# Reordering the last part of a four-layer network's first layer, and moving one group's channel scaling to ScalarE

## Chip, cores and metric

One Trainium2 chip, one core of it. The metric is the device time of one execution in microseconds, as the median of several runs.

## What is computed

The input x is 16 images of 64 channels and 16x16 pixels, float32. Four blocks follow one another, each as x = x + block(norm(x)), where norm is a group norm over pairs of channels:

```python
x = x + L0(gn(x))   # two dynamic convolutions, a 1x1 projection, channel and spatial attention
x = x + L1(gn(x))   # efficient attention and a three-level pyramid of channel attentions
x = x + L2(gn(x))   # 3x3 and 1x1 convolution mix
x = x + L3(gn(x))   # area attention, depthwise 5x5 and projection
```

The change lies in the last part of L0 and the first part of L1. The end of L0, after the second dynamic convolution (its product is y2):

```python
h = silu(bn2(y2))                       # 128 channels
h = silu(bn3(proj_w @ h))               # h3, 64 channels
a = sigmoid(mlp(mean(h)) + mlp(max(h))) # one number per image and channel: "channel gate"
h = h * a                               # h4
s = concat(mean over channels, max over channels)
x = x + h * sigmoid(conv7x7(s))         # one number per image and pixel: "map"
```

L1 begins with the norm, then products for keys, queries and values, exponentials, and two further levels of the image as differences of Gaussian blurs ("pyramid").

## The kernel before

An image pair is a tile t of 128 partitions (2 images x 64 channels) by 256 pixels; there are 8 tiles. They form two groups g = 0, 1 of four tiles, and within a group jj = 0, 1 counts two tiles (j = 2g + jj). Every engine has its own program, and all are written by walking one list, `SCHEDULE`: a list of steps such as `("h4T", jj, g)`, and every engine executes its own part of the step, if it has one, in that order. The list is built from `CHAIN`, in which group 1 runs three steps behind group 0. So the order of the list is the order of work on each engine, and an engine that waits in one step holds back all later steps on that engine. Nothing reorders at run time.

The steps around the change, with the parts of the engines and their lines:

- `y2` (L426, L1256): TensorE product of the second convolution; ScalarE silu (L1261) into h2.
- `y3` (L436, L921, L1264): TensorE projection (L442); ScalarE silu with a sum (L1267) into h3; VectorE maximum over pixels (L924).
- `mlp1` (L446, L927), `mlp2` (L454, L1278): the MLP's first product (L451), VectorE relu and add (L932, L935), second product (L457), ScalarE tanh (L1280) into `cag`.
- `h4T` (L460, L937): VectorE finishes the gate, 0.5 + 0.5 tanh (L942, with jj = 0 only), scales h3 by it (L945) into h4; TensorE transposes h4 to pixel-major (L468); VectorE sums and maxima over channels (L952).
- `conv7` (L471, L955, L1283): VectorE scales the sums (L958, `mean4`); TensorE multiplies by a 7x7 convolution as a matrix (L478); ScalarE tanh (L1285).
- `add` (L482, L960): TensorE spreads the map over channels (L413); VectorE adds to X (L964, L967) and takes the statistics of the next norm (L798, with jj = 1 also L805).
- `norm` 1: TensorE pair means (L353); VectorE variance (`gn_variance`, L814 to L816); POOL power -0.5 (L1470); VectorE coefficient (L824) and apply (L832) into xn1. `later_norm` (L839) puts these together.
- `in1` (L487, L1071, L1345): TensorE transposes (L495), keys (L498), queries and values (L505); VectorE maximum of the keys (L980), tokens (L1002), L994, L1012, L1013; ScalarE copy (L1298) and exponentials (L1293, L1313, L1327).
- `pyramid` (L509, L1316): sixteen 512-wide passes on TensorE (L517), copies on ScalarE (L1321).

TensorE's results go to PSUM banks in two rings, six for large and two for small products; `claim` (L330) takes the next bank and waits for the reader of what it held. The order of the claims is the order of the steps.

Part of the list before, from the first step that the change moves:

```python
("y2",0,1) ("mlp1",0) ("y3",0,1) ("mlp2",0) ("y2",1,1) ("h4T",0,0) ("y3",1,1) ("h4T",1,0)
("mlp1",1) ("conv7",0) ("mlp2",1) ("add",0,0) ("h4T",0,1) ("add",1,0) ("h4T",1,1) ("norm",1,0)
("conv7",1) ("in1",0,0) ("add",0,1) ("in1",1,0) ("add",1,1) ("pyramid",0) ("norm",1,1)
```

Of the kernel before, what the change touches and what calls it, by code (L numbers as in the profile page):

```python
# [25 lines left out]
NG = NP // 2  # L26
# [64 lines left out]
SCHEDULE = []  # L91
# [7 lines left out]

del SCHEDULE[SCHEDULE.index(("het", 0, 0)):]
SCHEDULE += [(*step, 1) for step in CHAIN[CHAIN.index(("norm", 2)) - LAG + 1:CHAIN.index(("norm", 2))]]
SCHEDULE += [("norm", 2, 1), ("het", 0, 0), ("het", 1, 0), ("norm", 3, 0), ("het", 0, 1), ("start3",), ("het", 1, 1)]
# [15 lines left out]
def program(nc, x_in, const_in, weight_in, param_in, out):  # L120
    F32 = mybir.dt.float32
    ALU = mybir.AluOpType
    ACT = mybir.ActivationFunctionType
# [8 lines left out]
    with ExitStack() as ctx:  # L132
# [8 lines left out]
        def bank(n, a=0, b=512):  # L141
            return psum[:, n * 512 + a:n * 512 + b]
# [29 lines left out]
        def sm(cols):  # L172
            small_bytes[0] += cols
            assert small_bytes[0] <= 1200
            return small[:, small_bytes[0] - cols:small_bytes[0]]
# [12 lines left out]
        mlp_s, cag = sm(NP), sm(NP)  # L188
# [21 lines left out]
        def pairs(cols=HW, layout="p (t n) -> p t n", axis=1, **sizes):  # L210

            n = NG * cols
            take(n)
            assert used[0] <= AREA_COLS // 2
            return ByGroup([region[:, at:at + n].rearrange(layout, t=NG, **sizes)
                            for at in (used[0] - n, AREA_COLS // 2 + used[0] - n)], axis)
# [6 lines left out]
        xs0, hs1, h3, h4, x_add = (pairs() for _ in range(5))  # L223
# [14 lines left out]
        xn1 = pairs()  # L238
# [12 lines left out]
        mix, mix2 = e_l[0], e_l[1]  # L251
# [527 lines left out]
        def _(dve):  # L779
            v = nc.vector  # L780
# [15 lines left out]
            def gn_stats(l, t, src_sem, value):  # L796
                dve.wait_ge(src_sem, value)
                v.bn_stats(stats[l][:, t, :], X[:, t, :]).then_inc(dve_small, 1)  # L798
                small_n[0] += 1
                stats_at[(l, t)] = small_n[0]  # L800

            def gn_aggr(l, g):
                for t in range(4 * g, 4 * g + 4):
                    dve.wait_ge(dve_small, stats_at[(l, t)])
                    v.bn_aggr(mv[l][:, t, :], stats[l][:, t, :]).then_inc(gn_mv[g], 1)  # L805
# [13 lines left out]
            def gn_coefs(l, g):  # L819
                dve.wait_ge(gn_pow[g], l + 1)  # L820
                n = where[("gn", l, g)]
                avg = bank(n, 0, 8).rearrange("p (t s) -> p t s", t=4)
                c = slice(4 * g, 4 * g + 4)
                v.scalar_tensor_tensor(out=gn_nb[l][:, c], in0=avg[:, :, 0], scalar=-1.0, in1=gn_rs[l][:, c],  # L824
                                       op0=ALU.mult, op1=ALU.mult).then_inc(gn_coef[g], 1)

            def gn_apply(l, t, dst):
                dve.wait_ge(gn_coef[t // NG], l + 1)
                src = X[:, t, :]
                if len(dst.shape) == 3:  # L830
                    src = src.rearrange("p (y x) -> p y x", y=W)
                v.tensor_scalar(dst, src, gn_rs[l][:, t:t + 1], gn_nb[l][:, t:t + 1], ALU.mult, ALU.add)\  # L832
                    .then_inc(xn_ready[t // NG], 1)
# [11 lines left out]
            def norm(l, g):  # L845
                if l == 0:
                    for t in range(NG * g, NG * (g + 1)):
                        gn_stats(0, t, x_loaded[t // 2], 16)
                    gn_aggr(0, g)
                    gn_variance(0, g)  # L850
                    gn_coefs(0, g)
                    c = slice(NG * g, NG * (g + 1))
                    v.tensor_tensor(xmean[:, c], gn_d[0][:, c], gn_rs[0][:, c], ALU.mult).then_inc(xmean_ready, 1)
                    for t in range(NG * g, NG * (g + 1)):
                        gn_apply(0, t, xn0[:, t, W:W + HW])
                elif l == 1:
                    later_norm(1, g, lambda t: xn1[:, t, :])
                elif l == 2:
                    dve.wait_ge(zero_ready, 2)
                    later_norm(2, g, lambda t: xn_pad[:, t, 1:17, 1:17])  # L860
                else:

                    dve.wait_ge(y1out_mm, NP)
                    later_norm(3, g, lambda t: xn3[:, t, :])
# [62 lines left out]
            def channel_mlp1(g):  # L927
# [6 lines left out]
                dve.wait_ge(mlp1_ready, 2 * g + 1)  # L934
                v.tensor_tensor(mlp_s[0:8, c], mlp_r[0:8, 0, c], mlp_r[0:8, 1, c], ALU.add).then_inc(mlp1_ready, 1)  # L935

            def tokens4(jj, g):  # L937
                j = 2 * g + jj
                if jj == 0:
                    own = cag[:, NG * g:NG * (g + 1)]  # L940
                    dve.wait_ge(cag_tanh, g + 1)
                    v.tensor_scalar(own, own, 0.5, 0.5, ALU.mult, ALU.add).then_inc(cag_ready, 1)  # L942
                dve.wait_ge(cag_ready, g + 1)
                for t in (2 * j, 2 * j + 1):
                    v.tensor_scalar(h4[:, t, :], h3[:, t, :], cag[:, t:t + 1], None, ALU.mult).then_inc(h4_ready, 1)  # L945

                dve.wait_ge(h4T_mm, j + 1)
                src = bank(where[("h4T", j)]).rearrange("p (q k b c) -> p q k b c", q=2, k=NK, b=2)
                for ch, op in ((0, ALU.add), (1, ALU.max)):
                    for q in range(2):  # L950
                        t = 2 * j + q
                        last = v.tensor_reduce(sT[:, ch, :, 2 * t:2 * t + 2], src[:, q, :, :, :], X_AXIS, op)  # L952
                    last.then_inc(sT_part, 1)

            def mean4(g):  # L955
                dve.wait_ge(sT_part, 4 * (g + 1))
# [222 lines left out]
            def add_out3(t):  # L1179
                dve.wait_ge(y3out_mm, t + 1)  # L1180
                dve.wait_ge(xt_ready, t + 1)
                if t >= 4:
# [3 lines left out]
                    .then_inc(yout_ready, 1)  # L1186

            steps = {"norm": norm, "ctx": context, "gate": gates, "spread": map_input,
                     "later_weights": later_weights, "y3": pool_max, "mlp1": channel_mlp1, "h4T": tokens4,
                     "conv7": mean4, "add": add0, "in1": in1, "levels": levels1, "scores1": scores1, "mix": mix1,  # L1190
                     "out1": out1, "het": het, "start3": first_keys}
            for name, *at in SCHEDULE:
                if name in steps:
# [3 lines left out]
            for w in range(NT + STEPS_MORE):  # L1197
                t, r = divmod(w, 4)
                j, r8 = divmod(w, 8)
# [25 lines left out]
        def _(act):  # L1225
            a = nc.scalar
# [51 lines left out]
            def channel_gate(g):  # L1278
                act.wait_ge(mlp2_mm, g + 1)
                a.activation(cag[:, NG * g:NG * (g + 1)], bank(where[("mlp2", g)], 0, NG), ACT.Tanh, scale=0.5)\  # L1280
                    .then_inc(cag_tanh, 1)

            def spatial_gate(g):  # L1283
                act.wait_ge(conv7_mm, g + 1)
# [134 lines left out]
            def second_blocks(l, g):  # L1419
                if l == 2:  # L1420
                    rows_of_groups(g, (2, 3))

            steps = {"norm": second_blocks, "gate": gates, "taps": taps_out, "conv": input_gate, "y1": silu1, "y2": silu2, "y3": silu3,
                     "mlp2": channel_gate, "conv7": spatial_gate, "in1": in1, "pyramid": pyramid_out,
                     "levels": levels1, "levels_T": levels_T, "scores1": scores1, "het": het_out, "start3": start3}
            for name, *at in SCHEDULE:
                if name in steps:
# [2 lines left out]
            for w in range(NT + 2):  # L1430
                j, r8 = divmod(w, 8)
# [301 lines left out]
```

## Time and profile before

| | |
|---|---|
| runs | 302.39, 304.10, 303.56 us; median 303.56 |
| profiled execution: time | 303.56 us |
| its span, first to last instruction | 301.8 us |
| TensorE busy | 228.6 us (76%) |
| VectorE busy | 187.1 us (62%) |
| ScalarE busy | 128.6 us (43%) |
| GpSimd (POOL) busy | 35.9 us (12%) |
| mean granted clock of TensorE | 0.869 of full |
| chain that ended last | PE 51%, DVE 23%, ACT 7%, issue 7%, DMA 5%, POOL 4% |

PE is TensorE's products, PEld its weight loads, DVE VectorE, ACT ScalarE. A busy share is an average over the whole span. The chain that ended last is followed back from the last instruction, at each step to what released it.
### The profile page before, as it was taken

Reading aid. Unit: us, or ns where it says so; the run is one execution under the profiler, and the core shown is the slowest. Engines: PE = TensorE matmul, PEld = TensorE weight load, DVE = VectorE, ACT = ScalarE, POOL = GpSimd, SP = SyncE. Lnnn points to the kernel's source line nnn. Section 1 sums busy time; section 2 is a strip of 40 time slices with the busy share of each in tenths; the row PEclk is TensorE's granted clock in tenths of the full one; section 3 lists DMA queues with packets and bytes.
Section 4 is the critical chain, followed back from the end, with each engine's and each line's share of the span. In section 5 each row is a group of like instructions: output and inputs, shape, how many; then the busy total and the mean of one; then the engine's idle time right before and its main releaser. Section 6 shows DMA issues by size and latency. Waiting matters only on the chain.

```text
span 301.8 us, 5842 instructions
## 1 busy us (share of the span) xinstructions
PE 228.6 (76%) x2192; PEld 133.9 (44%) x2192; DVE 187.1 (62%) x525; ACT 128.6 (43%) x322; POOL 35.9 (12%) x64
## 2 busy tenths in 40 slices
PE   0479897384399869988453679469989998988954
PEld 0355663132266546777321122234554564463541
DVE  3562343717449798398793036676497697697772
ACT  1025579400045577899300113336585465552410
POOL 1750000000100100000005022066020020000000
PEclk9996999855579999999755699958999999997995
DMA  7900000000000000000059951552034024100010
GB/s 231 393 0 3 0 2 1 0 0 2 0 0 0 3 0 0 2 3 2 1 138 211 217 121 36 129 120 67 0 80 101 2 66 117 45 6 21 0 37 35
DMA packets 9644, 16.54 MB, mean 55 GB/s; under 512 B 1936, under 2 KB 8208, under 8 KB 9360
## 3 DMA queue, kind: packets, MB, share of 16 engines
q1 hardware_dynamic: 8848, 13.58, 16.6%
q10 hardware_dynamic: 768, 2.58, 4.1%
q8 instruction: 18, 0.29, 0.4%
q14 instruction: 10, 0.08, 0.1%
HBM read 4.71 MB, written 1.05 MB: 19 GB/s over the span
## 4 chain that ended last, share of the span: by engine, by line
PE 51%; DVE 23%; ACT 7%; issue 7%; DMA 5%; POOL 4%; ACTq 2%; SPq 0%; DVEq 0%; POOLq 0%
PE psum L671 7%; PE psum L517 5%; PE psum L699 4%; DMA region<-xn_pad 4%; PE psum L717 4%; PE psum L689 3%; PE psum L651 3%; DVE xn_pad L1142 3%; DVE smax L1148 3%; POOL small L1470 2%; PE psum L478 2%; PE psum L413 2%; PE psum L505 2%; PE psum L633 2%; PE psum L388 2%
## 5 line engine op out<-in xcount | busy, mean ns | idle before, releaser
L1405 ACT ACTIVATE region<-psum 128x512 f32<-128x512 f32 x32 | 19.0, 593 | 32.7 <-PE psum L699 32.6
L1148 DVE TENSOR_REDUCE smax<-psum 128x8 f32<-128x512 f32 x32 | 21.8, 682 | 13.0 <-PE psum L689 13.0
L1470 POOL TENSOR_TENSOR small<-small 128x4 f32<-128x4 f32 x8 | 8.1, 1018 | 169.5 <-DVE small L816 169.5
L671 PE MATMUL psum<-region,w 128*32 128x512 f32 x160 | 22.6, 636 | 4.1 <-DVE region L1123 4.1
L1399 ACT ACTIVATE region<-region 128x512 f32<-128x512 f32 x32 | 20.1, 627 | 12.1 <-DVE region L1155 12.0
L798 DVE BATCH_NORM_STATS2 small<-X 128x6 f32<-128x256 f32 x32 | 12.5, 422 | 18.2 <-ACT X L1275 17.0
L699 PEld LDWEIGHTS psum<-const,region 128*128 128x128 f32 x128 | 14.9, 149 | 18.2 <-issue 12.1
L699 PE MATMUL psum<-const,region 128*128 128x128 f32 x128 | 21.9, 297 | 1.1 <-ACT region L1405 1.0
L1155 DVE TENSOR_TENSOR region<-psum,smax 128x512 f32<-128x512 f32 x32 | 22.0, 686 | 0.6
L717 PE MATMUL psum<-region 128*64 128x18 f32 x512 | 20.6, 214 | 0.0
L717 PEld LDWEIGHTS psum<-region 128*64 128x64 f32 x512 | 17.5, 138 | 5.4 <-issue 5.4
L1275 ACT ACTIVATE X<-psum,small 128x256 f32<-128x256 f32 x8 | 3.4, 470 | 37.2 <-PE psum L633 37.2
L633 PE MATMUL psum<-region,weight 128*32 128x512 f32 x96 | 12.7, 667 | 7.2 <-DMA region<-xn_pad 7.0
L651 PE MATMUL psum<-region,weight 128*128 128x512 f32 x24 | 13.9, 676 | 2.6 <-DVE small L824 2.6
L353 PE MATMUL psum<-small,const 128*128 128x8 f32 x16 | 4.0, 325 | 14.2 <-DVE small L805 10.0
L517 PE MATMUL psum<-region,const 128*128 128x512 f32 x32 | 14.2, 598 | 0.0
L1142 DVE SCALAR_TENSOR_TENSOR xn_pad<-v_pad,small,xn_pad 128x256 f32<-128x256 f32 x32 | 14.0, 483 | 0.0
L1285 ACT ACTIVATE region<-psum 8x256 f32<-8x256 f32 x2 | 0.7, 374 | 27.9 <-PE psum L478 27.9
L353 PEld LDWEIGHTS psum<-small,const 128*128 128x128 f32 x16 | 3.7, 284 | 17.5 <-DVE small L805 12.8
L689 PE MATMUL psum<-region 32*64 32x256 f32 x256 | 10.3, 433 | 1.3 <-ACT X L1275 1.3
L1298 ACT ACTIVATE region<-psum 128x512 f32<-128x512 f32 x20 | 11.0, 624 | 0.7 <-PE psum L495 0.7
L1518 POOL COPY region<-v_pad 128x256 f32<-128x256 f32 x16 | 6.3, 436 | 40.9 <-PE psum L660 37.1
(166 smaller groups left out, 472.5 us busy)
## 6 DMA issues: line engine op xcount, KB each, us to landing
region<-v_pad SPq DMA_DIRECT2D x64, 80.0 KB, 2.1
region<-xn_pad SPq DMA_DIRECT2D x16, 157.5 KB, 7.3
region<-xn_pad ACTq DMA_DIRECT2D x16, 157.5 KB, 7.2
weight<-weight_in SPq DMA_DIRECT2D x1, 1376.0 KB, 10.6
const<-const_in SPq DMA_DIRECT2D x1, 1170.0 KB, 7.9
X<-x SPq DMA_DIRECT2D x4, 256.0 KB, 4.4
out<-xn_pad SPq DMA_DIRECT2D x8, 128.0 KB, 1.7
weight<-weight_in SPq DMA_DIRECT2D x1, 918.0 KB, 5.0
```

Source lines behind the costliest of these rows:

```text
L517: last = mm(bank(n), lap[s][:, k, jn * 128:(jn + 1) * 128], xT[:, k, 4 * g:4 * g + 4, :].rearrange("p t c -> p (t c)"), start=(k == 0), st ...
L633: last = mm(bank(n)[32 * q:32 * q + 32, :], hetW[:, q % 2, dx, :], rows[:, q, 2 * jj:2 * jj + 2, 0:W, dx:dx + W], start=False, stop=(dx == 2),
L651: mm(bank(n), wt(w), xn3[:, 2 * j:2 * j + 2, :].rearrange("p t n -> p (t n)"), start=True, stop=True)\
L671: last = mm(bank(n)[32 * c:32 * c + 32, :], w4[:, c % 2, dx, :], v4[:, j % 2, c, :, :, dx:dx + W], start=(dx == 0), stop=(dx == 4), tile_p ...
L689: last = mm(bank(banks[r], a2 * 256, a2 * 256 + 256)[64 * c:64 * c + 64, :], q3[rows, j % 2, a, :], km[rows, j % 2, a, :, :].rearrange("p ...
L699: last = tr(bank(n, q * 128, (q + 1) * 128), e3[:, w % NE, q * 128:(q + 1) * 128], ident)
L717: last = mm(dst[half, a2, b, h:h + 2, :].rearrange("p h e -> p (h e)"), e3T[:, w % NE, at + 64 * c:at + 64 * c + 64], va[:, 4 * t + 2 * a2 ...
L1142: v.scalar_tensor_tensor(out=a, in0=win, scalar=pe_w[:, 5 * PE_ROWS + i:5 * PE_ROWS + i + 1], in1=prev, op0=ALU.mult, op1=ALU.add).then_in ...
L1148: v.tensor_reduce(smax[:, w, :], src, X_AXIS, ALU.max).then_inc(smax_ready, 1)
L1155: v.tensor_tensor(s_sub[:, w % NE, :].rearrange("p (h m) -> p h m", h=HEADS), src, smax[:, w, :].unsqueeze(2).broadcast_to([P, HEADS, AP_] ...
L1399: a.activation(e3[:, u % NE, :], s_sub[:, u % NE, :], ACT.Exp, scale=HD ** -0.5).then_inc(e3_ready, 1)
L1405: a.activation(e3T[:, u % NE, :], bank(where[("e3T", u)]), ACT.Copy).then_inc(e3T_ready, 1)
```

## The change

The 23 steps from `("y2", 0, 1)` up to `("levels", 0, 0)` get a new order by hand. The steps before and after keep theirs. In the new order both MLP steps of group 0 stand together and ahead of y2 of jj = 1, group 0's transposes, map product and both adds are ahead of group 1's transposes, `in1` of jj = 0 is ahead of group 1's map product, and group 1's adds stand together ahead of the pyramid.

On VectorE the gate's affine step moves from `h4T` to the step `mlp2`. `h4T` of group 0 scales and sums as before; of group 1 it does nothing on VectorE. The scaling of group 1 moves to ScalarE (`second_scaled`, four Copy activations with the gate as scale). The channel sums of group 1 and its `mean4` move into VectorE's part of `("norm", 1, 0)`: sums of jj = 0, then the variance, sums of jj = 1, `mean4`, then coefficient and apply.

```diff
--- before.py
+++ after.py
@@ -99,6 +99,12 @@
 
 
 
+TAIL = [("y2", 0, 1), ("mlp1", 0), ("mlp2", 0), ("y2", 1, 1), ("h4T", 0, 0), ("y3", 0, 1), ("h4T", 1, 0), ("y3", 1, 1), ("conv7", 0),
+        ("mlp1", 1), ("mlp2", 1), ("add", 0, 0), ("add", 1, 0), ("h4T", 0, 1), ("h4T", 1, 1), ("norm", 1, 0), ("in1", 0, 0),
+        ("conv7", 1), ("in1", 1, 0), ("add", 0, 1), ("add", 1, 1), ("pyramid", 0), ("norm", 1, 1)]
+first, beyond = SCHEDULE.index(TAIL[0]), SCHEDULE.index(("levels", 0, 0))
+assert sorted(SCHEDULE[first:beyond]) == sorted(TAIL)
+SCHEDULE[first:beyond] = TAIL
 del SCHEDULE[SCHEDULE.index(("het", 0, 0)):]
 SCHEDULE += [(*step, 1) for step in CHAIN[CHAIN.index(("norm", 2)) - LAG + 1:CHAIN.index(("norm", 2))]]
 SCHEDULE += [("norm", 2, 1), ("het", 0, 0), ("het", 1, 0), ("norm", 3, 0), ("het", 0, 1), ("start3",), ("het", 1, 1)]
@@ -853,6 +859,15 @@
                     v.tensor_tensor(xmean[:, c], gn_d[0][:, c], gn_rs[0][:, c], ALU.mult).then_inc(xmean_ready, 1)
                     for t in range(NG * g, NG * (g + 1)):
                         gn_apply(0, t, xn0[:, t, W:W + HW])
+                elif l == 1 and g == 0:
+
+                    map_sums(0, 1)
+                    gn_variance(1, 0)
+                    map_sums(1, 1)
+                    mean4(1)
+                    gn_coefs(1, 0)
+                    for t in range(NG):
+                        gn_apply(1, t, xn1[:, t, :])
                 elif l == 1:
                     later_norm(1, g, lambda t: xn1[:, t, :])
                 elif l == 2:
@@ -934,16 +949,21 @@
                 dve.wait_ge(mlp1_ready, 2 * g + 1)
                 v.tensor_tensor(mlp_s[0:8, c], mlp_r[0:8, 0, c], mlp_r[0:8, 1, c], ALU.add).then_inc(mlp1_ready, 1)
 
+            def channel_gate(g):
+                dve.wait_ge(cag_tanh, g + 1)
+                own = cag[:, NG * g:NG * (g + 1)]
+                v.tensor_scalar(own, own, 0.5, 0.5, ALU.mult, ALU.add).then_inc(cag_ready, 1)
+
             def tokens4(jj, g):
+
+                if g == 0:
+                    dve.wait_ge(cag_ready, 1)
+                    for t in (2 * jj, 2 * jj + 1):
+                        v.tensor_scalar(h4[:, t, :], h3[:, t, :], cag[:, t:t + 1], None, ALU.mult).then_inc(h4_ready, 1)
+                    map_sums(jj, 0)
+
+            def map_sums(jj, g):
                 j = 2 * g + jj
-                if jj == 0:
-                    own = cag[:, NG * g:NG * (g + 1)]
-                    dve.wait_ge(cag_tanh, g + 1)
-                    v.tensor_scalar(own, own, 0.5, 0.5, ALU.mult, ALU.add).then_inc(cag_ready, 1)
-                dve.wait_ge(cag_ready, g + 1)
-                for t in (2 * j, 2 * j + 1):
-                    v.tensor_scalar(h4[:, t, :], h3[:, t, :], cag[:, t:t + 1], None, ALU.mult).then_inc(h4_ready, 1)
-
                 dve.wait_ge(h4T_mm, j + 1)
                 src = bank(where[("h4T", j)]).rearrange("p (q k b c) -> p q k b c", q=2, k=NK, b=2)
                 for ch, op in ((0, ALU.add), (1, ALU.max)):
@@ -951,6 +971,10 @@
                         t = 2 * j + q
                         last = v.tensor_reduce(sT[:, ch, :, 2 * t:2 * t + 2], src[:, q, :, :, :], X_AXIS, op)
                     last.then_inc(sT_part, 1)
+
+            def conv7(g):
+                if g == 0:
+                    mean4(0)
 
             def mean4(g):
                 dve.wait_ge(sT_part, 4 * (g + 1))
@@ -1186,8 +1210,8 @@
                     .then_inc(yout_ready, 1)
 
             steps = {"norm": norm, "ctx": context, "gate": gates, "spread": map_input,
-                     "later_weights": later_weights, "y3": pool_max, "mlp1": channel_mlp1, "h4T": tokens4,
-                     "conv7": mean4, "add": add0, "in1": in1, "levels": levels1, "scores1": scores1, "mix": mix1,
+                     "later_weights": later_weights, "y3": pool_max, "mlp1": channel_mlp1, "mlp2": channel_gate, "h4T": tokens4,
+                     "conv7": conv7, "add": add0, "in1": in1, "levels": levels1, "scores1": scores1, "mix": mix1,
                      "out1": out1, "het": het, "start3": first_keys}
             for name, *at in SCHEDULE:
                 if name in steps:
@@ -1280,6 +1304,12 @@
                 a.activation(cag[:, NG * g:NG * (g + 1)], bank(where[("mlp2", g)], 0, NG), ACT.Tanh, scale=0.5)\
                     .then_inc(cag_tanh, 1)
 
+            def second_scaled(jj, g):
+                if g == 1:
+                    act.wait_ge(cag_ready, 2)
+                    for t in (NG + 2 * jj, NG + 2 * jj + 1):
+                        a.activation(h4[:, t, :], h3[:, t, :], ACT.Copy, scale=cag[:, t:t + 1]).then_inc(h4_ready, 1)
+
             def spatial_gate(g):
                 act.wait_ge(conv7_mm, g + 1)
                 a.activation(gate_map[g][0:GB, :], bank(where[("conv7", g)], 0, HW)[0:GB, :], ACT.Tanh, scale=0.5)\
@@ -1421,7 +1451,7 @@
                     rows_of_groups(g, (2, 3))
 
             steps = {"norm": second_blocks, "gate": gates, "taps": taps_out, "conv": input_gate, "y1": silu1, "y2": silu2, "y3": silu3,
-                     "mlp2": channel_gate, "conv7": spatial_gate, "in1": in1, "pyramid": pyramid_out,
+                     "mlp2": channel_gate, "h4T": second_scaled, "conv7": spatial_gate, "in1": in1, "pyramid": pyramid_out,
                      "levels": levels1, "levels_T": levels_T, "scores1": scores1, "het": het_out, "start3": start3}
             for name, *at in SCHEDULE:
                 if name in steps:
```

## Rows read from the trace of the kernel before

**Rows 1.** The cores: span and mean granted clock of TensorE.

```profile
core 0: 301.8 us, clock 0.869
```

**Rows 2.** Chain of waits, 50 to 104 us: start, length (us), what.

```profile
55.01 1.21 ACT region L1267 x4
...
60.32 3.58 PE psum L478 x8
...
64.41 2.03 PE psum L413 x4
...
81.15 3.58 PE psum L478 x8
...
88.66 1.06 PE psum L413 x4
...
94.00 7.06 PE psum L517 x16
```

**Rows 3.** Stretches of 1 us: length; busy PE, PEld, DVE, ACT, POOL; clock; DMA.

```profile
58.00:59.00 1.00, 0.00 (x0) 0.00 (x0) 0.99 (x3) 0.00 (x0) 0.00 (x0) 0.91 0.00 0
86.00:87.00 1.00, 1.00 (x5) 0.48 (x4) 0.09 (x1) 0.98 (x2) 0.00 (x0) 0.94 0.00 0
171.00:172.00 1.00, 1.00 (x12) 0.14 (x7) 0.00 (x0) 0.00 (x0) 0.00 (x0) 0.77 1.09 217
```

**Rows 4.** Timeline from 168 us, TensorE (columns as in rows 5).

```profile
168.26 3.92 PE L633 MATMUL psum<-region,weight 128*32 128x512 f32 x20 [7.02 <-DMA region<-xn_pad]
```

**Rows 5.** Timeline, 50 to 60: start, length, engine, line, what, count, [idle before].

```profile
49.55 1.47 ACT L1261 ACTIVATE region<-psum,small 128x256 f32<-128x256 f32 x3
...
50.38 0.15 DVE L935 TENSOR_TENSOR small<-small 8x4 f32<-8x4 f32 x1
...
51.65 0.38 PE L457 MATMUL psum<-small,weight 8*128 8x4 f32 x2
...
51.96 1.14 PE L434 MATMUL psum<-region 64*128 64x256 f32 x8
...
52.75 1.93 ACT L1261 ACTIVATE region<-psum,small 128x256 f32<-128x256 f32 x4 [0.27 <-PE psum L434]
...
53.25 0.62 DVE L945 TENSOR_SCALAR region<-region,small 128x256 f32<-128x256 f32 x2
...
54.31 1.08 PE L442 MATMUL psum<-region,weight 128*64 128x256 f32 x8
54.42 1.42 DVE L952 TENSOR_REDUCE small<-psum 128x4 f32<-128x256 f32 x4 [0.55 <-PE psum L468]
...
56.25 0.69 DVE L924 TENSOR_REDUCE small<-region 128x2 f32<-128x512 f32 x1 [0.41 <-ACT region L1267]
...
57.34 0.63 PE L468 MATMUL psum<-const,region 128*128 128x128 f32 x4 [1.95 <-DVE region L945]
```

**Rows 6.** Timeline, 60 to 82, VectorE.

```profile
72.40 0.69 DVE L964 SCALAR_TENSOR_TENSOR region<-psum,region 128x512 f32<-128x512 f32 x1 [0.58 <-PE psum L413]
...
74.53 0.36 DVE L805 BATCH_NORM_AGGREGATE small<-small 128x2 f32<-128x6 f32 x4
...
76.40 1.42 DVE L952 TENSOR_REDUCE small<-psum 128x4 f32<-128x256 f32 x4 [1.01 <-PE psum L468]
...
79.43 0.16 DVE L824 SCALAR_TENSOR_TENSOR small<-psum,small 128x4 f32<-128x4 f32 x1 [1.15 <-POOL small L1470]
79.63 1.38 DVE L832 TENSOR_SCALAR region<-X,small 128x256 f32<-128x256 f32 x4
```

**Rows 7.** Timeline, 82 to 92, ScalarE and VectorE.

```profile
86.42 1.28 ACT L1293 ACT_TABLE_LOAD   x1
...
86.91 0.69 DVE L980 TENSOR_REDUCE small<-psum 128x2 f32<-128x512 f32 x1 [5.82 <-PE psum L498]
...
90.21 0.51 ACT L1313 ACTIVATE region<-region,small 128x256 f32<-128x256 f32 x1 [1.03 <-DVE small L995]
...
91.41 0.68 DVE L964 SCALAR_TENSOR_TENSOR region<-psum,region 128x512 f32<-128x512 f32 x1
```

## The prediction

> **What bounds the kernel now.** I read the cores first: the span is 301.8 us [rows 1], the run that was profiled took 303.56 us, which is also the median of the three runs, so 1.76 us lie around the span and a change of the span can be taken off 303.56 directly. Then the chain of waits, from 60 to 102 us [rows 2]. It shows this stage as one serial string with TensorE in most of it: the 7x7 map product of the first group (conv7(0), L478) at 60.32, the spreading of that map (L413) at 64.41, the same map product for the second group at 81.15, and from there TensorE without a break to the end of the pyramid (L517) at 94.00 + 7.06 = 101.06. The next stage starts from the second group's means behind the pyramid on TensorE, so what ends the stage is how soon that unbroken block of TensorE work can begin.
>
> The granted clock is the second thing to see [rows 3]. It drops to 0.50 (1.2 GHz) at about 58.8 (mean 0.91 in that microsecond) and is back at 2.4 GHz at about 86.1. All the products between run at half speed. Before the drop TensorE had mostly been idle; the rise came 4.9 us into the unbroken block (81.15 to 86.06).
>
> Between 66 and 81 us the string goes through VectorE: first group's add, second group's scaling and channel sums, add, sums, norm, each waiting for TensorE in turn [rows 6].
>
> **The sum, part 1: to conv7(0).** Times are of the trace's own clock. The MLP's second product (L457, 0.38) now stands right behind the first: its input is ready at 50.53, so it ends at 50.95 instead of 52.03 behind y3(0,1) [rows 5]. ScalarE is in silus until 51.02, then the gate's tanh, done 51.2. On VectorE the gate's affine step follows (0.2 with its wait, as L935's 0.15), and from the scaling (L945, 53.25) to the first channel sum (L952, 54.42) it is 1.17 us, so the sums could start at 52.6; the transposes queue behind y2(1,1) (1.14, from 50.95 to 52.1), which makes it 52.8, and sums of 1.42 end at 54.2. ScalarE: silu2(1,1), 1.93, ends at 53.2; the two silus of y3(0,1), 1.21 with their reads [rows 2], at 54.45. Pool maximum 0.69, to 55.2. From the start of the scaling at 53.25 to the end of the sums at 55.84 it is 2.6, so jj = 1 is through at 57.8. But y3(1,1) (1.08) is now behind those transposes on TensorE, from 56.3 (the transposes, 0.63, end 1.5 before the sums do) to 57.4; its silus end 0.7 later at 58.1, the maximum at 58.8, the mean at 59.0, conv7(0) starts at 59.07. That is 1.25 earlier than 60.32, where undoing the queue behind the transposes would have allowed 58.
>
> **Part 2: to the first add.** Both MLP products of the second group stood before or beside conv7(0); now both come after it on TensorE. conv7(0) ends at 62.65 (3.58 at the low clock); mlp1 (0.2), VectorE's two small steps (0.45) and mlp2 (0.5, which is what lies between 63.90 and 64.41 [rows 2]) bring the spreading to 63.8 instead of 64.41, its first map done 2.1 later, the add to 65.9 instead of 66.5. Of the 1.25 us, 0.65 is given back. The channel gate of group 1 is a wait on VectorE with the adds queued behind it; its tanh ends at 64.1, and they wait for the spreading until 65.9 anyway: no cost. The map's tanh is ahead of it on ScalarE and done by then.
>
> **Part 3: the scaling on ScalarE.** Four Copy activations with a scale from SBUF, 128x256, SBUF to SBUF. No row shows this form; the nearest is the exponential of the same size, SBUF to SBUF, 0.51 each [rows 7], the other bound is 1.93 / 4 = 0.48 for a silu of that size from PSUM [rows 5]. Four take 2.0 and run from 64.35 to 66.4 while ScalarE has nothing else. TensorE comes to them at 67.95, so up to 0.9 each would cost nothing. VectorE is spared two pairs of 0.6.
>
> **Part 4: adds and sums on VectorE.** One add with its statistics takes 2.13 (72.40 to 74.53) [rows 6]. The two now run on end, since the spreading of jj = 1 ends at 67.95: 65.9 to 70.2, aggregation 0.36, 70.55. Before, the second add only began at 72.40. TensorE meanwhile does the transposes of the second group (0.63 each at the full clock [rows 5], at most twice that at the low one, to 70.5) and the small product of the means, to 71. The first sums take 1.42, to 71.95, variance 0.5 (77.82 to 78.3, where VectorE's 1.15 of waiting for POOL begins), and that wait is now covered by the second sums, 1.42 to 73.9. Mean and coefficient 0.35, apply from 74.3 instead of 79.63: 5.33 earlier. No order on POOL or SP changes, and no DMA is issued by a moved step.
>
> **Part 5: the block on TensorE.** in1(0,0) now goes ahead of conv7(1). It needs two of four applies (1.38 for the four [rows 6]) and 0.1 to reach TensorE, so it starts 0.8 after 74.3, at 75.1; before, the block started at 81.15: 6.05 earlier. The block holds the same instructions, 19.9 us of which 4.9 at the low clock. TensorE counts as the bound if nobody stalls it. VectorE: the keys' product before landed at 86.91, 2.2 after conv7(1)'s end at 84.73, the last 0.8 at full clock; all low makes it 3.0, so 78.1. in1 takes VectorE 4.5 (86.91 to 91.41) [rows 7], plus up to 0.8 of waiting for slow products: 83.4. ScalarE's exponential of the queries then ends at 84.1 and the second map's tanh, which now sits behind it, at 84.5. TensorE wants that map after in1(0,0), conv7(1) and in1(1,0). The first two took 81.15 to 88.66 [rows 2], 7.5; with 0.4 less for the clock (below) they end at 82.2, and in1(1,0) took 94.00 - 1.05 - 89.72 = 3.2: 85.4. Slack 0.9. VectorE takes in1(1,0) from at most 84.4 to 88.9, two adds to 93.1, aggregation 93.5; the pyramid ends at 94.6. Slack 1.1. The banks that the pyramid takes over are read by 86.2 at the latest. So TensorE bounds it.
>
> The clock in the block: the rise came 4.9 us after the start, of which 3.58 was a product with weights 8 columns wide; in another place it came 3.1 us after (TensorE starts at 168.26 [rows 4], rise in the microsecond from 171 [rows 3]) with wide work. Now wide products come first. I take 4.1, half of the 0.8 difference is 0.4 us gained. Bounds: 3.1 gives 0.9 gained. From above, conv7(0) and the spreading ran 6.1 us on end (60.32 to 66.44) with no rise, so 7.5 is possible: 1.3 us lost against 4.9.
>
> As to a rule: the transposes of in1 open the block. The Trainium skill, "TensorE: Matmul & The Clock Gate", Part 4, says that transposes do not engage the full clock as products do. By that the rise would come about 1 us later and the sum be 0.5 us smaller; the trace has transposes at 84.73 inside a low stretch and the rise 1.3 later, which fits both.
>
> And a second rule, on ScalarE: the second map's tanh now stands between exponentials. The trace has one table load, 1.28, ahead of the first exponential [rows 7]. If tanh needs another table, two more loads come in: 84.5 becomes 85.8, TensorE waits 0.4, and the reload falls before the exponential of the second keys, whose bank the pyramid needs at 89.3, so the bound for this is 0 to 0.4 us. I take 0: the tanhs between the silus of this stage already run without a load of their own (the load in [rows 7] is the stage's only one). The Trainium skill, "ScalarE: Activation LUTs", Table sets, has tanh and exp in one set, by which it is 0; no row here shows a tanh after an exponential.
>
> **Sum:** 6.05 + 0.4 = 6.45 us earlier at the end of the pyramid. Nothing after it changes its order, and it all hangs on that chain, so 303.56 - 6.45 = 297.1.
>
> **Rivals.**
> *The clock falls later (B).* TensorE was idle for 1.95 us before 57.34, worked 0.63 and then had only mlp1 before 60.32 [rows 2, 5]; at 58.8 the clock fell. Now y3(1,1) adds 1.08 us there and conv7(0) starts at 59.07. If 2.4 GHz survives to conv7(0)'s end, that takes 1.8 us instead of 3.6 and the small products 0.3 less: 2.1 more gained, 295.0; through the spreading too, 2.9 and 294.2. For it: the work that fills the gap. Against: between 53.8 and 59.1 it still has no more than 1.7 us of work.
>
> *The rise comes late (C).* 7.5 us instead of 4.1 into the block: 1.7 less gained, 298.8. One us late, if transposes do not serve, costs 0.5 (297.6) and lies in the forecast's own range; it has a third of the forecast's chance. VectorE then also gets its products later, but adds still end before the pyramid. For it: the 6.1 us without a rise; against: those were narrow products.
>
> *Slower (D).* The half clock holds through the block. The block is 19.9 - 2.45 = 17.5 us at full clock. It ends at 75.1 + 17.5 + half the low time; it is later than before once the low time passes 17 us; if all is low it ends at 110 and the kernel takes 312.5. The only mechanism that I find with a price above the 6 us gained. Against: every block of wide work here got its clock within 5 us.
>
> *It does not do what it says (E).* The adds could be held by something I read as free (a gate late on ScalarE, scaling far over 0.9 each): the apply stays near 79 and the time within 1.5 us of 303.
>
> **How the numbers follow.** Forecast 0.50, B 0.25, C 0.15, D 0.05, E 0.05. Range: B with the clock bound of 3.1 at the low end, 293.9; C with the 0.9 us by which the runs of before differ, 299.6; the forecast's own range is 296.2 to 298.3. A measurement tells about 0.5% (1.5 us) from no change; faster by more than that are the forecast, B and C and a part of E: 0.92, same 0.03, slower 0.05.
>
> **What would show it.** Right: conv7(0) near 59.1, first add near 65.9, second on its heels, apply near 74.3, in1(0,0) on TensorE near 75.1 and before conv7(1), end of pyramid near 94.6, still three table loads, four activations near 0.5 us between 64 and 67. Wrong: a wait of TensorE for ScalarE's tanh before the spreading of group 1; VectorE's adds ending after the pyramid; a low clock past 80; later stages that take longer than before.

## The result and the profile after

The changed kernel takes 293.45 us (292.95 to 294.38, four runs) beside 303.41 us before: ratio 0.9678, 95% interval 0.964 to 0.9715. That is 10 us saved where 6.5 were forecast, and 0.45 us below the low end of the range. Some executions of a kernel take over 1.5% longer than its fastest; the ratios here leave these out, the medians and ranges of times hold all executions. The profiled execution of the changed kernel took 294.38 us with a span of 292.6 us; its mean granted clock is 0.894 beside 0.869. The page's span line, busy times and chain:

```profile
span 292.6 us, 5842 instructions
...
PE 223.4 (76%) x2192; PEld 132.7 (45%) x2192; DVE 186.3 (64%) x521; ACT 130.5 (45%) x326; POOL 35.9 (12%) x64
...
PE 50%; DVE 24%; ACT 8%; issue 6%; DMA 5%; POOL 4%; ACTq 2%; SPq 0%; DVEq 0%; POOLq 0%
```

TensorE has the same 2192 instructions but is busy for 5.2 us less (223.4 beside 228.6): the same work ran faster. The chain of waits of the changed kernel, 50 to 100 us (start, length, what), the pieces that answer to [rows 2] and to the sum's steps:

```profile
52.09 1.93 ACT region L1285 x4
54.02 1.10 ACT region L1291 x4
...
56.24 1.07 PE psum L474 x4
57.31 1.93 PE psum L448 x8
...
60.77 1.89 PE psum L484 x8
...
64.57 0.70 DVE region L988
...
72.56 0.75 DVE region L838 x2
...
73.35 1.11 PE psum L501 x4
...
78.29 1.82 PE psum L484 x8
...
85.27 7.06 PE psum L523 x16
...
93.13 1.02 POOL small L1500
```

L474 are the transposes of h4, L448 is y3, L484 the map product conv7, L988 the first add, L838 the apply, L501 the transposes of in1, L523 the pyramid. The pyramid ends at 92.33 instead of 101.06. conv7(0) starts at 60.77, no earlier than before, but takes 1.89 us, not 3.58; the first add is at 64.57, the apply at 72.56, and the block starts at 73.35. The granted clock in the four microseconds in which it moves (columns as in [rows 3]):

```profile
56.00:57.00 1.00, 0.76 (x4) 0.69 (x4) 0.36 (x2) 0.00 (x0) 0.00 (x0) 0.63 0.00 0
59.00:60.00 1.00, 0.21 (x2) 0.00 (x0) 0.06 (x1) 0.71 (x3) 0.00 (x0) 0.66 0.00 0
66.00:67.00 1.00, 0.42 (x4) 0.18 (x2) 0.97 (x3) 0.00 (x0) 0.00 (x0) 0.75 0.00 0
76.00:77.00 1.00, 1.00 (x7) 1.00 (x6) 0.76 (x2) 0.40 (x1) 0.00 (x0) 0.63 0.00 0
```

In this execution it falls at about 56.3, under the transposes (1,0) and y3(1,1), which take 1.07 and 1.98 instead of 0.63 and 1.08. It is back at 59.7, ahead of conv7(0), stays through the spreading, falls at 66.5 and rises 3.4 us into the block, at 76.7. Group 1's activations and the table loads on ScalarE (busy, mean ns, idle before):

```profile
L1311 ACT ACTIVATE region<-region,small 128x256 f32<-128x256 f32 x4 | 1.7, 500 | 0.2 <-DVE small L955 0.2
...
L1256 ACT ACT_TABLE_LOAD x1 | 1.3, 1283 | 0.7 <-PEq L1756 0.7
L1276 ACT ACT_TABLE_LOAD x1 | 1.3, 1283 | 1.7 <-PE psum L429 1.7
L1323 ACT ACT_TABLE_LOAD x1 | 1.3, 1283 | 0.0
```

Four at 0.50 each, near the 0.51 of the forecast, and hidden. There are still three loads, though the second map's tanh (81.70) now stands between exponentials (80.36 and 82.86), so a tanh behind an exponential wants none. That is as the Trainium skill has it ("ScalarE: Activation LUTs", Table sets), and now shown.

**A length that can be compared.** The code ahead of the first moved step is unchanged, yet it starts between 46.9 and 49.6 us: near 47 in the three profiles whose mean granted clock over the first 44 us is 1.00, near 49 where it is 0.92. What lies behind the pyramid takes 199.6 to 203.5 us, though nothing is changed there. So the runs below are also read by the tail: from the first silu of y2(0,1) on ScalarE to the end of the pyramid on TensorE. Before it is 49.08 to 101.06, 51.98 us; the forecast made it 45.5 (94.6 - 49.08); the changed kernel has 42.84. Of the kernel before there is one profile, so its tail stands on one execution.

### The profile page after: what moved, and what is told of

The parts are those of the page before. It is cut to its first block, busy times and chain, and to the rows that moved or that the text cites. A ratio compares the mean times of both kernels' runs of the same rounds, so it can differ in the third digit from the quotient of the medians.

```text
span 292.6 us, 5842 instructions
## 1 busy us (share of the span) xinstructions
PE 223.4 (76%) x2192; PEld 132.7 (45%) x2192; DVE 186.3 (64%) x521; ACT 130.5 (45%) x326; POOL 35.9 (12%) x64
## 4 chain that ended last, share of the span: by engine, by line
PE 50%; DVE 24%; ACT 8%; issue 6%; DMA 5%; POOL 4%; ACTq 2%; SPq 0%; DVEq 0%; POOLq 0%
PE psum L677 7%; PE psum L523 5%; PE psum L705 4%; DMA region<-xn_pad 4%; PE psum L723 4%; PE psum L695 3%; PE psum L657 3%; DVE xn_pad L1166 3%; DVE smax L1172 3%; POOL small L1500 2%; PE psum L511 2%; PE psum L639 2%; ACTq L1446 2%; PE psum L429 2%; ACT region L1367 2%
## 5 line engine op out<-in xcount | busy, mean ns | idle before, releaser
L804 DVE BATCH_NORM_STATS2 small<-X 128x6 f32<-128x256 f32 x32 | 12.5, 422 | 18.2 <-ACT X L1299 16.9
L639 PE MATMUL psum<-region,weight 128*32 128x512 f32 x96 | 12.5, 658 | 7.3 <-DMA region<-xn_pad 7.3
L657 PE MATMUL psum<-region,weight 128*128 128x512 f32 x24 | 13.9, 676 | 2.6 <-DVE small L830 2.6
L1328 ACT ACTIVATE region<-psum 128x512 f32<-128x512 f32 x20 | 10.9, 624 | 8.8 <-PE psum L501 8.8
L523 PE MATMUL psum<-region,const 128*128 128x512 f32 x32 | 14.2, 598 | 0.0
L639 PEld LDWEIGHTS psum<-region,weight 128*32 128x32 f32 x96 | 2.9, 120 | 17.1 <-DMA region<-xn_pad 9.7
## 6 DMA issues: line engine op xcount, KB each, us to landing
weight<-weight_in SPq DMA_DIRECT2D x1, 1376.0 KB, 10.9
```

What stands on the lines that cost most here:

```text
L523: last = mm(bank(n), lap[s][:, k, jn * 128:(jn + 1) * 128], xT[:, k, 4 * g:4 * g + 4, :].rearrange("p t c -> p (t c)"), start=(k == 0), st ...
L639: last = mm(bank(n)[32 * q:32 * q + 32, :], hetW[:, q % 2, dx, :], rows[:, q, 2 * jj:2 * jj + 2, 0:W, dx:dx + W], start=False, stop=(dx == 2),
L657: mm(bank(n), wt(w), xn3[:, 2 * j:2 * j + 2, :].rearrange("p t n -> p (t n)"), start=True, stop=True)\
```

## The experiments

What is to be told apart: the order's own gain from the clock's, and the parts of the order from one another. Ratios are against the kernel before on the same chip.

### Clock held by dummy products

```diff
+def keep_busy(n, times):
+    for _ in range(times):
+        mm(bank(n, 256, 512), ident, lap[1][:, 0, :], start=True, stop=True)
...
 n = claim(pe, ("h4T", j), sT_part, 2 * j + 2)
+keep_busy(n, {(1, 0): 4}.get((jj, g), 0))
```

The dummies write the bank that the step has claimed, and the step overwrites it. In the changed kernel there are 4 before the transposes (1,0), 6 before group 0's means and 7 before in1(0,0), 17 in all. In the kernel before there are 3, 5 and 5 before the transposes (1,0), (0,1) and (1,1), 3 before mlp1(1) and 9 before conv7(1). Where a step waited before it claimed its bank, the claim is moved ahead of the wait.

> The kernel before with dummy products in TensorE's idle stretches between 55 and 81 us (3 to 9 products of 128x256 into the bank that the step claims anyway), so that the clock should stay at 2.4 GHz; the result isn't touched. Clock theory (much of the change's gain beyond 6 us is that the 7x7 product and the spreading now run at full clock): all the work between 58.8 and 86.1 that ran at half speed, 1.8 + 1.0 + 0.5 + 1.0 + 0.5 + 1.8 + 0.6 = 7.2 us on the chain, comes back: about 296.3 us. Order theory (the clock is incidental, the order gave it all): the dummies cost a little and return nothing, 303 to 305 us.

296.72 us, ratio 0.9788 (0.9752 to 0.9823), 6.2 us under the kernel before on that chip. Its profile has no half clock in the tail, which is 45.40 us.

> The changed kernel with dummy products in TensorE's idle stretches before the transposes (1,0), before the means and before in1(0,0). Clock theory: transposes and y3(1,1) at 56 to 59 us (1.4 us too long) and the first 3.1 us of the block (1.5 us too long) run at full clock, 290.6 us; and the distance to filled_before, 5.7 us, is then the order's own share. Order theory: at or above the changed kernel's 293.4 us.

290.08 us, ratio 0.958 (0.9535 to 0.9626), tail 39.98.

> filled_after once more, beside the others on one chip, 289.5 to 291 us: the changed kernel with dummy products in three idle stretches of TensorE. Clock theory: tail 39.9 us with no half clock in it.

291.60 us, ratio 0.9682 (0.9646 to 0.9718), tail 39.98 again. The clock in four microseconds that were low in a profile of the changed kernel or in that of the kernel before:

```profile
53.00:54.00 1.00, 1.00 (x5) 0.57 (x3) 0.77 (x2) 0.20 (x2) 0.00 (x0) 1.00 0.00 0
58.00:59.00 1.00, 1.00 (x7) 0.44 (x5) 0.00 (x0) 0.00 (x0) 0.00 (x0) 1.00 0.00 0
66.00:67.00 1.00, 0.93 (x5) 0.88 (x6) 1.00 (x5) 0.00 (x0) 0.00 (x0) 1.00 0.00 0
70.00:71.00 1.00, 0.79 (x5) 0.69 (x6) 0.80 (x3) 0.10 (x1) 0.00 (x0) 1.00 0.00 0
```

> filled_after without the four dummies before the transposes (1,0). Clock theory: of the 2.9 us, only the 1.5 of the block's first stretch is had in executions where the clock falls at 56 us (those lose up to 1.3), all of it in the others: 290 to 292 us, tail 41.4 us if the profile shows the half clock before conv7(0), 39.9 if not. If the dummies after the spreading don't matter: 293.4 us and tail 42.8.

290.85 us, ratio 0.9675 (0.9624 to 0.9725), tail 39.99 in a profile without half clock in it.

With the clock held the change saves 45.40 - 39.98 = 5.4 us. The clock costs the kernel before 51.98 - 45.40 = 6.6 us of its tail and the changed kernel 2.9. So 3.7 of the 9.1 us of the tail are clock; with the tail of after_third below (41.97) they are 4.6 of 10.0. The times of the two filled kernels, taken on one chip, are 6.6 us apart (296.72 and 290.08), 1.2 more than their tails; that part lies outside the tail and is not explained. The order theory, by which the dummies return nothing, is out for the kernel before. For the changed kernel the gain of the dummies alone is seen in the tail only: its runs without them are of other chips, and the ratios of the three filled versions (0.958, 0.9682, 0.9675) reach up to its own 0.9678. The one comparison on one chip is at the end of the experiments, with conv7(1) moved.

### Which work sits ahead of conv7(0)

```diff
-("h4T", 1, 0), ("y3", 1, 1), ("conv7", 0)
+("y3", 1, 1), ("h4T", 1, 0), ("conv7", 0)
```

> The changed kernel with y3(1,1) ahead of the transposes (1,0). By order alone, the wait of y3 behind the transposes goes and conv7(0) starts 1.1 us earlier: 292.3 us. Clock theory: TensorE's back-to-back stretch at 56 to 59 us, which brought the clock up again at 59.4, is gone, so conv7(0) and the spreading run at half clock (1.8 + 1.0 us more): 294 to 295 us, with the clock at 0.50 under conv7(0) in the profile.

297.24 us, ratio 0.9808 (0.9773 to 0.9843); conv7(0) takes 3.45 us; tail 44.64.

> y3(1,1) ahead of the transposes (1,0), second profile. If TensorE's back-to-back stretch ahead of conv7(0) is what holds or brings the clock: conv7(0) at the half clock again, 3.5 us, tail 44 to 46 us, time 2 to 4 us above after_third. If it was luck: 1.9 us under conv7(0), a tail near 42 and the time of after_third.

296.66 us, ratio 0.9839 (0.9773 to 0.9905); tail 44.99. TensorE's timeline of this one. Between the 2.4 us without work and the 1.7 us ahead of conv7(0) stand only the transposes, 0.63 us, where the changed kernel has y3(1,1) as well:

```profile
52.53 1.95 PE L448 MATMUL psum<-region,weight 128*64 128x256 f32 x16
56.91 0.63 PE L474 MATMUL psum<-const,region 128*128 128x128 f32 x4 [2.44 <-DVE region L962]
59.26 3.58 PE L484 MATMUL psum<-weight,small 128*8 128x256 f32 x8 [1.72 <-DVE small L982]
```

> The changed kernel as it is, once more, for a second profile and six more times. If the clock's pattern in the tail is fixed by the work, the profile shows the same fall near 56 and rise near 59; if it depends on how the execution happens to lie against the clock's steps (my theory, after map_first had none of it in the same code), it shows another, and the times spread over 2 us or so around 293.4 us.

294.42 us (291.51 to 298.00), ratio 0.9705 (0.9637 to 0.9774); conv7(0) 1.89 us; tail 42.83.

> The changed kernel, third profile. If the full clock under conv7(0) is the rule: conv7(0) takes 1.9 us and the tail 41.5 to 42.9 us, time 292 to 294.5 us. If it was luck: 3.5 us and a tail of 44.5 to 46 us in this one.

293.29 us, ratio 0.9716 (0.9651 to 0.9781); tail 41.97. Here the clock does not even fall at 56; y3 behind the transposes is followed by conv7(0) at 1.7 us distance (TensorE's timeline):

```profile
52.44 0.66 PE L474 MATMUL psum<-const,region 128*128 128x128 f32 x4
53.03 1.08 PE L448 MATMUL psum<-region,weight 128*64 128x256 f32 x8
56.32 0.63 PE L474 MATMUL psum<-const,region 128*128 128x128 f32 x4 [2.21 <-DVE region L962]
56.88 1.08 PE L448 MATMUL psum<-region,weight 128*64 128x256 f32 x8
59.64 1.89 PE L484 MATMUL psum<-weight,small 128*8 128x256 f32 x8 [1.68 <-DVE small L982]
```

So in three of three profiles the changed kernel has conv7(0) at the full clock and in two of two the swap has it at half, with the time 3.4 us higher on the same chip (296.66 beside 293.29). It is not certain in each execution. Ten profiles of this section and the next ones have the changed kernel's order up to conv7(0) and no dummies ahead of it; in nine conv7(0) takes 1.89 us, and in the tenth, sums_first below, it is at half:

```profile
55.74 0.63 PE L474 MATMUL psum<-const,region 128*128 128x128 f32 x4 [2.20 <-DVE region L962]
56.30 1.97 PE L448 MATMUL psum<-region,weight 128*64 128x256 f32 x8
59.83 3.48 PE L484 MATMUL psum<-weight,small 128*8 128x256 f32 x8 [1.56 <-DVE small L982]
```

The swap was also a test of my reading that y3(1,1) is held up by the transposes. conv7(0) starts 10.2 us into the tail, where after_third has 10.08: nothing is gained. VectorE's timeline in y3_first_again shows why: the second maximum (L939) is now ahead of the scaling (L962) that the transposes wait for, and it waits for a silu until 55.82.

```profile
54.73 0.69 DVE L939 TENSOR_REDUCE small<-region 128x2 f32<-128x512 f32 x1 [0.67 <-ACT region L1291]
55.82 0.69 DVE L939 TENSOR_REDUCE small<-region 128x2 f32<-128x512 f32 x1 [0.41 <-ACT region L1291]
56.42 0.61 DVE L962 TENSOR_SCALAR region<-region,small 128x256 f32<-128x256 f32 x2
...
65.90 0.69 DVE L988 SCALAR_TENSOR_TENSOR region<-psum,region 128x512 f32<-128x512 f32 x1 [1.54 <-PE psum L419]
```

The last line is the first add. It starts 65.90 - 49.06 = 16.8 us into the tail, to which the half clock through conv7(0) and the spreading brings it; the forecast's sum, made with that clock, had 16.8 too.

### The parts

The first kernel is the one before with the change's list and nothing else:

```diff
+TAIL = [("y2", 0, 1), ("mlp1", 0), ("mlp2", 0), ("y2", 1, 1), ("h4T", 0, 0), ("y3", 0, 1), ("h4T", 1, 0), ("y3", 1, 1), ("conv7", 0),
+        ("mlp1", 1), ("mlp2", 1), ("add", 0, 0), ("add", 1, 0), ("h4T", 0, 1), ("h4T", 1, 1), ("norm", 1, 0), ("in1", 0, 0),
+        ("conv7", 1), ("in1", 1, 0), ("add", 0, 1), ("add", 1, 1), ("pyramid", 0), ("norm", 1, 1)]
```

> The kernel before with the new order of the 23 steps and nothing else: VectorE keeps group 1's scaling, and its sums stand in h4T, ahead of the norm. Against the changed kernel VectorE's string gets two scalings (0.6 each), two waits for transposes (0.5 to 1.0 each) and the POOL wait (1.15) back: 4 to 5 us, so 297.5 to 298.5 us. If the scaling and the sums are incidental and the order gave it all: 294 us.

303.67 us (299.67 to 308.11), ratio 0.9953 (0.9908 to 0.9999), tail 53.16. The profile is of an execution of 304.71 us, and the twelve go down to 299.67, so 53.16 may be a long tail for this kernel; the ratio is the safer measure. A miss, and the expectation had left something out. TensorE and VectorE:

```profile
77.87 1.12 PE L501 MATMUL psum<-const,region 128*128 128x128 f32 x4 [3.82 <-DVE region L838]
...
80.48 3.45 PE L511 MATMUL psum<-weight,region 128*128 128x128 f32 x16
86.92 3.49 PE L484 MATMUL psum<-weight,small 128*8 128x256 f32 x8 [2.98 <-DVE small L964]
```

```profile
86.08 0.69 DVE L1019 TENSOR_TENSOR region<-region,small 128x512 f32<-128x512 f32 x1
86.69 0.17 DVE L964 TENSOR_SCALAR small<-small 128x16 f32<-128x16 f32 x1
```

The 0.17 us step is the mean of group 1's sums (L964). In the list it belongs to conv7(1), and in the new order that is behind in1(0,0) on VectorE too. TensorE, through with in1(0,0) at 83.9, stands for 3 us until that small step comes. Beside the changed kernel's first profile the string from the first add to the apply is 4.5 us longer (77.08 - 64.60 = 12.5 beside 8.0), which is the 4 to 5 us expected, and the block 5.8 longer (24.8 beside 19.0): 3.0 of waiting, 1.6 as the clock falls at the end of that wait (87.0) and conv7(1) takes 3.49 for 1.89, the rest a later rise. So moving the mean into the norm isn't bookkeeping; the order by itself is worth 0.5% (0 to 0.9).

The second is the changed kernel with group 1's scaling back on VectorE and with the sums ahead of the variance:

```diff
-gn_variance(1, 0)
 map_sums(1, 1)
 mean4(1)
+gn_variance(1, 0)
...
+for t in (NG + 2 * jj, NG + 2 * jj + 1):
+    v.tensor_scalar(h4[:, t, :], h3[:, t, :], cag[:, t:t + 1], None, ALU.mult).then_inc(h4_ready, 1)
...
-        a.activation(h4[:, t, :], h3[:, t, :], ACT.Copy, scale=cag[:, t:t + 1]).then_inc(h4_ready, 1)
```

> The changed kernel with group 1's scaling back on VectorE and both sums and the mean ahead of the variance: that is, the new order plus the second map's mean moved ahead of VectorE's in1(0,0), nothing else. order_alone had that mean behind in1(0,0), and TensorE stood until it came. If that was why the order alone gained nothing: the tail (from the silus of y2(0,1) to the end of the pyramid) is 1.6 + 1.2 us longer than the changed kernel's 42.8, about 46, and the time 296.5 to 298.5 us. If the new order gives nothing by itself: 302 to 304 us.

296.07 us, ratio 0.9821 (0.9784 to 0.9857), tail 44.99. So the order with the mean in its place gives 7.0 of the 9.1 us of tail, clock included. It differs from order_alone in more than the mean: all four scalings now stand ahead of all sums, and its string from the first add to the apply is 10.9 us beside 12.5 (73.68 - 62.83). By the ratios, 0.9821 beside 0.9953, the place of the mean and that of the scalings are worth about 4 us together; the 8 us between the two tails rest on that one long execution.

The next two undo one part each, the scaling's engine (its line goes into VectorE's part of h4T) and the place of the variance:

```diff
-a.activation(h4[:, t, :], h3[:, t, :], ACT.Copy, scale=cag[:, t:t + 1])
+v.tensor_scalar(h4[:, t, :], h3[:, t, :], cag[:, t:t + 1], None, ALU.mult)
```

> The changed kernel with group 1's scaling back on VectorE, between the adds and the norm. It puts 1.2 us of scaling and up to 1.5 us of waiting for the first transposes into the string, less 0.3 of the wait that is there: 295.0 to 296.0 us. If ScalarE's share is hidden anyway: 293.4 us.

295.71 us, ratio 0.9799 (0.9746 to 0.9851), tail 44.31. From the second step of the second add (L991 in the changed kernel) to the apply it is 72.61 - 65.83 = 6.8 us beside 72.56 - 67.40 = 5.2: 1.6 more, the least that was expected.

```diff
 map_sums(0, 1)
-gn_variance(1, 0)
 map_sums(1, 1)
 mean4(1)
+gn_variance(1, 0)
```

> The changed kernel with both sums and the mean ahead of the variance, so that POOL's power is uncovered. The wait of 1.15 us comes back into the string: 294.6 us, apply 1.2 us later after the adds than in the changed kernel. If VectorE or TensorE had that slack elsewhere: 293.4 us.

296.43 us, ratio 0.9809 (0.9759 to 0.9858), tail 45.95. The same stretch is 74.45 - 68.06 = 6.4 us, 1.2 longer than in the changed kernel, as expected. Of the rest of the 3.1 us of tail, 1.6 is conv7(0) at the half clock in that profile. The time missed the expected 294.6 by 1.8 us; whether the executions without a profile had that half clock too isn't known.

### The second map's place, and the fastest version

```diff
-("norm", 1, 0), ("in1", 0, 0), ("conv7", 1), ("in1", 1, 0)
+("norm", 1, 0), ("conv7", 1), ("in1", 0, 0), ("in1", 1, 0)
```

> The changed kernel with only conv7(1) put back ahead of in1(0,0) on all engines. The block can start 0.9 us earlier, as it wants the second map's sums and no apply. If the clock rises as soon for a narrow product: 292.5 us. If the narrow product does not bring it (my theory, rise at 4.9 us instead of 3.1): the 0.9 us is given back and VectorE gets its keys 2 us later, so 293.4 to 294.0 us.

291.56 us, ratio 0.9616 (0.9574 to 0.9658), tail 41.17. The rise came 4.6 us into the block, as in the second case, and the time is below both cases: a miss.

> conv7(1) ahead of in1(0,0), second profile. By the sum (block starts 0.85 earlier, its narrow product is the one that runs at the half clock, 0.4 us longer): 0.5 us under after_third, tail 41 to 42.5 us. If its first result was the luck of the clock: equal to after_third.

292.61 us, ratio 0.9706 (0.9647 to 0.9765), tail 41.27. On that chip it is 0.7 us under after_third (293.29), within what the runs differ by. Against after_third's tail of 41.97, also without a half clock ahead of conv7(0), it is 0.7 to 0.8 shorter.

> filled_after with conv7(1) back ahead of in1(0,0), dummies before it instead of before in1(0,0). With the clock held, the block starts 0.85 us earlier and is equally long, VectorE gets the first keys 1.0 us later and its adds end at about the pyramid's end: tail 39.3 us against 39.9, time 0.6 us under filled_again. If VectorE becomes the bound: equal to it or slower.

The dummies here are 16: 4, 6, and 6 before conv7(1). 290.41 us, ratio 0.9618 (0.9572 to 0.9664), tail 39.03.

> Dummy products in the idle stretches and conv7(1) ahead of in1(0,0): tail 39.0 us as before, 3.8 us under the changed kernel's, so 2.5 to 4 us under after_third in time. If the dummies give back later what they gain in the tail: 0 to 1.5 us under it.

289.71 us, ratio 0.9615 (0.956 to 0.9671), tail 39.04: 3.6 us under after_third on the same chip (289.24 to 291.07 beside 291.23 and more, no overlap), and 2.9 us under map_first_again, the same list without dummies on that chip. This beats both kernels: dummy products in the idle stretches, and the second map again ahead of in1(0,0).

## Why the prediction missed

The forecast's mechanism held and its size did not. The direction and all order steps are right; the step that failed is the choice between the forecast and its own rival B: "conv7(0) ends at 62.65 (3.58 at the low clock)", with B, the clock staying up through the spreading, at a chance of 0.25. The runs show 1.89 us for conv7(0), not 3.58, in all three profiles of the changed kernel, and 1.97 us at most for both parts of the spreading, where the sum had 2.05 for each. B's own mechanism, a clock that falls later, is seen in one of the three, after_third; in the other two the clock fell as the transposes (1,0) began (at 56.3 and 53.8) and was back before conv7(0) started (59.7 and 57.8). Where the clock is at half through both, in y3_first_again, the sum fits: first add 16.8 us in, as forecast, and a tail of 44.99 beside 45.5.

- **Part 1, conv7(0) 9.99 us into the tail** (59.07 - 49.08). 10.08 in after_third. In the first profile it is 11.28, as y3(1,1) and its transposes ran at half speed there. Right, but "undoing the queue behind the transposes would have allowed 58" is wrong: y3_first gained nothing, for VectorE's maximum takes the place of TensorE's queue.
- **Part 2, first add 16.8 us in.** The sum had 3.58 us of conv7(0) and 2.05 of spreading at the half clock. Measured 64.57 - 49.49 = 15.1, and 13.9 in after_third (63.49 - 49.56). B's sentence took off 2.9: 13.9. The term was mis-sized, not the order.
- **Part 3, scaling hidden, 0.51 each.** 0.50 each, nothing waits. Worth 1.6 us of VectorE's string (scale_dve).
- **Part 4, 8.4 us from first add to apply** (74.3 - 65.9). 72.56 - 64.57 = 8.0. Right.
- **Part 5, block starts 0.8 after the apply's start; TensorE is the bound.** 0.79, and TensorE runs from 73.35 to 92.33 without a stop: 18.98 us. The forecast said 19.5. The rise came 3.4 us in, not 4.1. Slack for the second map's tanh and for VectorE's adds was enough. The chance that tanh wants a table: no.
- **Narrow products and the rise.** I thought that conv7(1) at the head of the block would delay the rise. map_first has it there, 3.6 us at half speed, and the rise 4.6 us in; other profiles have it anywhere from 3.3 to 6.1 us in (after_again and y3_first, 5.6 in scale_dve) with the same wide work. The two can't be told apart by this. Nor by conv7(0): the clock rose 3.2 us into it in sums_first (59.83 to 63.08), while in y3_first_again TensorE worked from 59.26 to 69.47 on the same product, the spreading and transposes with one gap of 0.5 us, all of it at half. So the time to the rise is not fixed by the work, as the forecast took it to be. Whether the transposes of in1 delay the rise, as would follow from the Trainium skill ("TensorE: Matmul & The Clock Gate", Part 4), no run here shows.
- **C, D, E** did not come. E's mechanism is real all the same: order_alone is held by a step that I read as free, the mean, and the change escapes it only because it moves that step.

Put together, the tail of 45.5 less B's 2.9 is 42.6, and 42.0 to 42.8 were measured. The range's low end, 293.9, was B with the early rise for one execution of 303.56; by the forecast's own terms (294.2, and 0.9 in place of 0.4 for the rise) it should have been 293.7, and its own range 296.6 to 298.8 in place of 296.2 to 298.3. It took no account of how much the rest of the kernel moves with the clock: the time before alone went from 298.9 us (granted clock 0.895) to 305.6 (0.863) over 54 runs. The profiled execution, 294.38 us, is 0.2 from B's 294.2; it is the slowest of the four. Why their median is 0.7 us below B isn't settled by a run.

## What to carry to other kernels

Closing TensorE's idle stretches ahead of half-speed work pays twice, by the wait and by the clock: here 5.4 us and 3.7. Cost a reorder at both clock levels, and ask which work now lies right ahead of the products; a swap that looks free may open the gap again. In a list that all engines share, look for small steps that belong to a moved name: one of 0.17 us, queued behind a long step of its own engine, made TensorE wait 3.0 us, and the clock fell at the end of that wait.

## What was not expected of the hardware

- The same code at the same place has another clock pattern in each execution: in their first 100 us the changed kernel's three profiles have low stretches from 22, 32, 56 and 66 us, from 53 and 64, and from 21, 31 and 66.
- 16 dummy products of 128x256, 7.6 us of TensorE's time with no use, made the same list 2.9 us faster (292.61 to 289.71), as they ran where it would have been idle.
- A small difference in time between two orders needs several profiles: the ratio of the same dummy version was 0.958 on one chip and 0.9682 on another, while its tail was 39.98 us in both.
